# Attention output kept transposed and undivided in DRAM, divided by the output projection

## What is computed

```python
q = (x @ Wq.T + bq).reshape(b, l, h, hd).transpose(0, 2, 1, 3)      # k, v alike
scores = jnp.einsum('bhqd,bhkd->bhqk', q, k) / math.sqrt(hd)
scores = jnp.where(causal, scores, -jnp.inf)
att = jax.nn.softmax(scores, axis=-1)
out = jnp.einsum('bhqk,bhkd->bhqd', att, v)
out = out.transpose(0, 2, 1, 3).reshape(b, l, d)
return out @ Wo.T + bo                                              # x = x + this
```

## Time and profile before

| | us |
|---|---|
| median of 3 runs (1972.41 to 1987.93) | 1975.94 |
| the profiled execution's own time | 1980.81 |
| its span in the trace | 1979.0 |
| first row `mxT` written (slot 0 may start) | 169.40 |
| row `mxT` of slot 15 written | 589.19 |
| end of the last `add` of the output projection | 669.92 |
| first instruction of the MLP phase | 672.4 |

### The profile page before, as it was taken

One profiled execution on the slowest core, in us unless ns is written; L12 is line 12 of the kernel. 1 busy time (PEld: TensorE's weight loads), 2 busy tenths in 40 slices (PEclk: granted clock), 3 DMA queues, 4 the chain that ended last, 5 costly groups with the idle time before them and its releaser, 6 DMA issues.

```text
span 1979.0 us, 39339 instructions
## 1 busy us (share of the span) xinstructions
PE 1836.3 (93%) x14968; PEld 1122.2 (57%) x14968; DVE 1462.5 (74%) x2302; ACT 1031.1 (52%) x1888; POOL 760.7 (38%) x922
## 2 busy tenths in 40 slices
PE   7998888888889798999999998999999999989979
PEld 3443333333333476775775766666676766747746
DVE  6567688888873313997988988887889889969821
ACT  4234677777774123654654645636646546536411
POOL 4685656566772111223215224142151151322331
PEclk9998899999999898999999999999999999999989
DMA  7864544556434604006132331234232142071010
GB/s 237 233 198 139 153 120 126 141 140 182 142 110 118 207 1 126 12 12 188 36 125 50 81 125 41 90 81 143 68 105 73 40 133 73 12 201 33 12 40 12
DMA packets 217131, 205.68 MB, mean 104 GB/s; under 512 B 136400, under 2 KB 173264, under 8 KB 216992
## 3 DMA queue, kind: packets, MB, share of 16 engines
q1 hardware_dynamic: 210992, 187.77, 33.3%
q0 software_dynamic: 4272, 12.91, 2.0%
q10 hardware_dynamic: 1728, 3.15, 0.4%
HBM read 147.39 MB, written 33.62 MB: 91 GB/s over the span
## 4 chain that ended last, share of the span: by engine, by line
PE 51%; DVE 6%; issue 3%; POOL 3%; DMA 2%; ACT 1%; SPq 0%; DVEq 0%; ACTq 0%
PE ga L1507 12%; PE ub L1507 12%; PE acc L1517 12%; PE ga L1535 5%; PE ub L1535 5%; PE acc L1550 4%; DVE junk L1651 1%; DMA pp<-ax 1%; POOL ax L1469 1%; POOL pp L1463 1%; DVE kept L1701 1%; DVE h L1708 1%; POOL lohi L1453 1%; DMA ring<-wgu_scr 0%; DVE pat L1655 0%
## 5 line engine op out<-in xcount | busy, mean ns | idle before, releaser
L1453 POOL TENSOR_TENSOR lohi<-h,lohi 128x256 f16<-128x256 f32 x224 | 176.4, 788 | 737.8 <-ACT lohi L1598 737.6
L1587 ACT ACTIVATE kept<-ax,T 128x1376 f16<-128x1376 f32 x248 | 357.0, 1439 | 170.5 <-DVE T L1657 166.7
L1651 DVE TENSOR_SCALAR_CACHE_REDUCE junk<-ax,T 128x1376 f16<-128x1376 f32 x248 | 406.4, 1639 | 3.3
L1067 ACT ACTIVATE pr<-s 128x512 f32<-128x512 f32 (+2 forms) x640 | 320.2, 553 | 96.1 <-PE s L956 75.5
L649 DVE TENSOR_REDUCE mx<-s 128x2 f32<-128x1024 f32 (+2 forms) x300 | 319.9, 1113 | 65.3 <-PE s L628 34.7
L1507 PE MATMUL ga<-xT_f,w_gate 128*128 128x256 f16 x2688 | 332.8, 274 | 17.8 <-DVE h L1708 13.6
L1507 PE MATMUL ub<-xT_f,w_up 128*128 128x256 f16 x2688 | 332.6, 274 | 0.0
L1517 PE MATMUL acc<-w_down,lohi 128*128 128x512 f16 x1344 | 326.4, 379 | 3.9 <-POOL lohi L1453 3.9
L1507 PEld LDWEIGHTS ga<-xT_f,w_gate 128*128 128x128 f16 x2688 | 262.7, 98 | 95.0 <-DVE h L1708 21.3
L1507 PEld LDWEIGHTS ub<-xT_f,w_up 128*128 128x128 f16 x2688 | 264.3, 98 | 31.6
L1708 DVE SCALAR_TENSOR_TENSOR h<-ub,g 128x256 f32<-128x256 f32 x224 | 93.8, 419 | 155.0 <-ACT g L1593 154.0
(11 more groups left out here) (179 smaller groups left out, 2670.5 us busy)
## 6 DMA issues: line engine op xcount, KB each, us to landing
ring<-wgu_scr SPq DMA_DIRECT2D x64, 688.0 KB, 5.3
ring<-wd_scr SPq DMA_DIRECT2D x24, 768.0 KB, 6.1
wgu_scr<-tk_h POOLq DMA_DIRECT2D x32, 172.0 KB, 2.7
q_scr<-qk_h SPq DMA_DIRECT2D x16, 256.0 KB, 2.5
k_scr<-qk_h SPq DMA_DIRECT2D x16, 256.0 KB, 4.0
v_scr<-v_f SPq DMA_DIRECT2D x16, 256.0 KB, 5.1
Q<-q_scr SPq DMA_DIRECT2D x64, 64.0 KB, 2.1
K<-k_scr SPq DMA_DIRECT2D x64, 64.0 KB, 2.0
```

The costliest lines, as they stand in the source:

```text
L1067: nc.scalar.activation(pr[:, g % NPR, NP * t + p0:NP * t + p1, 0:w], scores, ACT.Exp, scale=SCALE).then_inc(e2_ok, 1)
L1453: nc.gpsimd.tensor_tensor(hT[j % 2][:, 1, :], h[j % 2][:, :], hT[j % 2][:, 0, :], ALU.subtract).then_inc(hl_ok, 1)
L1587: nc.scalar.activation(kept[0][:, :], ax[k % 2][:, 1, 0:I_TK], ACT.Sign, scale=-1.0, bias=TF[:, 1:2], accum_out=cnt[:, 1:2]).then_inc(c1_o ...
L1651: nc.vector.tensor_scalar(junk[:, :], ax[k % 2][:, 0, 0:I_TK], TF[:, 0:1], -float(KZERO), ALU.is_lt, ALU.add, accum_out=cnt[:, 0:1]).then_ ...
```

## The change

- `copy_out` no longer feeds a transpose. SP stores `oT` as it is, one DMA for each half, into `o_scr`, now (slot, 128 rows, 1024 tokens): 16 rows of undivided output and 16 of sums for each head. `output_transpose`, `divide`, `o_st` and the per-tile `rows` on PE are gone; the next half's first product waits for `copy_out` alone, and `copy_out` waits for the store of the slot before.
- For each batch and half (a quarter, q = 0 to 3) SP loads the sums of 32 heads and 512 tokens as a 128 x 128 tile (`load_sums`, four DMAs), DVE inverts it (`invert`), and SP stores the result to a new scratch `r_scr` (`store_over`, four DMAs).
- The projection goes in 8 groups of 256 tokens. `load_group` issues 16 DMAs on SP: eight load 16 partitions of output each, features on partitions, and eight load the inverses, one row broadcast to 16 partitions. DVE multiplies the two (`rows`), ACT or DVE makes the high part, DVE the low part, and PE runs the products for two tiles, now with four PSUM tiles.
- The slot's order string is another. ACT peels slot 1 off its loop and DVE slots 13 and 14, with `invert(0)` and `invert(1)` behind them.

```diff
-            def store(n):
...
+            def store(n, f):
+                sp.wait_ge(oc_ok, 2 * n + f + 1)
+                sp.dma_start(o_scr[n, :, f * BANK:(f + 1) * BANK], oT[:, f, :]).then_inc(o_out[f], 16)
...
+            def load_sums(q):
+                b, f = q // 2, q % 2
+                wait(sp, over_out[f], 16 * NSEG * b)
+                sp.wait_ge(o_out[f], 16 * GPB * (b + 1))
+                rows = o_scr[b * GPB:(b + 1) * GPB].rearrange("n (j r) t -> (n j) r t", j=QH)[:, HD, :]
+                for c in range(NSEG):
...
+                    sp.dma_start(sums[c * H:(c + 1) * H, q % 2, :], rows[:, t0:t0 + P]).then_inc(sums_in[f], 16)
+            def store_over(q):
+                b, f = q // 2, q % 2
+                sp.wait_ge(over_ok, q + 1)
+                for c in range(NSEG):
...
+                    sp.dma_start(r_scr[b, :, t0:t0 + P], sums[c * H:(c + 1) * H, q % 2, :]).then_inc(over_out[f], 16)
+            def load_group(u):
+                b, q, i = u * GW // L, u * GW // BANK, u % 2
+                wait(sp, lo_ok, u - 1)
+                sp.wait_ge(o_out[q % 2], 16 * GPB * (b + 1))
+                sp.wait_ge(over_out[q % 2], 16 * NSEG * (b + 1))
...
+                for e in range(2):
+                    for j in range(QH):
...
+                        sp.dma_start(ov[i][p, :, :], values[e, j, 0:HD, :, :]).then_inc(o_ld[i], 16)
+                        sp.dma_start(osr[i][p, :, :], over[m].unsqueeze(0).broadcast_to([HD, KB, GW])).then_inc(o_ld[i], 16)
...
             for n in range(NQ):
+                if n:
+                    store(n - 1, 1)
+                store(n, 0)
...
+                if n == NQ - 4:
+                    load_sums(0)
+                    load_sums(1)
                 if n == NQ - 2:
...
+                    store_over(0)
+                    store_over(1)
+                    load_group(0)
+                    load_group(1)
+            load_sums(2)
+            load_group(2)
+            load_group(3)
+            store_x(0)
+            store_x(1)
+            store_over(2)
+            load_group(4)
+            store_x(2)
+            store_x(3)
+            load_group(5)
+            store(NQ - 1, 1)
+            load_sums(3)
+            store_over(3)
+            for u in range(6, NGRP):
+                load_group(u)
...
             def product(t, k):
                 if k == 0:
-                    pe.wait_ge(lo_ok, t + 1)
+                    pe.wait_ge(lo_ok, t // TPG + 1)
...
-                wait(act, ot_ok, 2 * n + f - 1)
+                wait(act, o_out[f], 16 * n)
...
+            for t in range(NTILE):
+                u = t // TPG + 2
                 add(t)
+                if t == 1:
+                    invert(2)
+                if t == 5:
+                    invert(3)
+                if t % TPG and u < NGRP:
+                    rows(u)
...
-TENSOR_ORDER = "mmrmrsmrsmmssrsmrsmmsrrmsrsmmsrsmmsrsmmsrsmmsrmsmsrsmrs"
+TENSOR_ORDER = "mmrrmsmsmsmsmsmrsmmsrsmrrsmmsrsmmsrsmmsrsmmsrsmsrsmrs"
```

More of the change, by code:

```diff
@@ L719, in phase_attend @@
         XBESIDE = NDB * 3
[L720 to L721 removed]
+        pmm = [s1[i // 2][:, i % 2 * BANK:(i % 2 + 1) * BANK] for i in range(NPM)]
         va_ok = sem("va_ok")
@@ L742, in phase_attend @@
         xb_ok = sem("xb_ok")
-        tr_ok = sem("ctr_ok")
+        ov_ok = sem("cov_ok")
+        sums_in = [sem(f"sums_in{i}") for i in range(2)]
+        over_ok = sem("over_ok")
+        over_out = [sem(f"over_out{i}") for i in range(2)]
         hi_ok = [sem(f"chi_ok{i}") for i in range(2)]
@@ L773, in phase_attend @@
         order = attend_order(N1, len(pairs2), NG, end_av)
[L776 to L779, removed]
+        steps = [("product", t, k) for t in range(EARLY) for k in range(KB)]
         def last_order():
@@ L1007, in slot @@
                         products(n - 1, 1 - i, a)
-                    elif kind == "output":
-                        output_transpose(n, 0)
-                    elif kind == "output before" and not first:
-                        output_transpose(n - 1, 1)
                     elif kind == "maxima":
@@ L1079, in _ @@
             slot(0, first=True)
-            with act.Fori(1, NQ) as n:
+            slot(1)
+            with act.Fori(2, NQ) as n:
                 slot(n)
@@ L1116, in slot @@
                         sc.maxima(dve, s1, n + 1, a)
-                    elif kind == "output":
-                        divide(n, 0, h, i)
-                    elif kind == "output before" and not first:
-                        divide(n - 1, 1, h if i else h - 1, 1 - i)
                     elif kind == "maxima end":
@@ L1180, in attend_order @@
     shifted = [("shifted", v) for v in range(n2)]
-    rest = [("products before", g) for g in range(ng - TENSOR_LATE, ng)] + [("output before", 1)]
-    rest += [("products", g) for g in range(end_av[0])] + [("output", 0)]
-    rest += [("products", g) for g in range(end_av[0], ng - TENSOR_LATE)]
+    rest = [("products before", g) for g in range(ng - TENSOR_LATE, ng)]
+    rest += [("products", g) for g in range(ng - TENSOR_LATE)]
     queues = {"m": maxima, "s": shifted, "r": rest}
```

184 lines of the change are left out of this document (67 added, 117 removed).

## The result

The changed kernel took 2019.07 us (median of 4 runs, 2013.09 to 2021.59) against 1974.18 for the kernel before: ratio 1.0212, 95% interval 1.0187 to 1.0237. It is 2.1% slower. The forecast was 1983 us and its range ended at 2012.

The account below looks back on a forecast made before the run. No engine is full: PE, DVE and ACT, nearly full, hand work to each other. 1980.81 - 22.5 (slots) + 29.8 (tail) = 1988.1 us for the profiled execution, 4.9 above the median: 1983 us, range 1953 to 2012.

Parts of the forecast that it names:

- the slots: 15 slots up to the last mxT write: 1.5 us gained in each, 22.5 us in sum, bounds 12 and 45.
- the tail: From the last mxT write (called E) to the last add: 29.8 us longer, 110.5 instead of 80.7, bounds +16 and +53.
- the next slot's row is on its way as much earlier: Slot's end: with DVE earlier, the next row of maxima starts as much earlier; part of the 0.8 us gain.
- DVE sets the end of a slot: Slot's end: PE's maxima transpose waits for DVE's join and the last shifted pair queues behind it, ACT idling 0.69 us.
- the 0.8 forecast for the slot's end: Slot's end: DVE 1.4 us earlier without divisions, of which 0.8 us a slot is gained, ACT and PE then setting the pace.
- the 0.7 forecast for the first third: Slot's first third: new order saves 0.4 us of ACT's 0.62 gap, missing transposes 0.3 more; about 0.7 us a slot.
- the wait ahead of tile 0: Tail, slot 15: PE waits 13.9 us for group 0 to be loaded and split, where before it transposed at once.
- the second wait: Tail, behind tile 7: PE idle 21 us, as group 4's multiplication stands on DVE behind invert(3).
- landing of 2.1 us: Tail: a load lands 2.1 us after its issue, and the same was used for stores.
- The first (transfers): Rival, tail: narrow group loads are bound by transfer, not issue; 7 x 3.3 = 23 us more, 2006 us; chance 0.16.
- The second (clock falls): Rival, slot's first third: new string lets PE's clock fall; in the other 11 slots +44, 2027 us; chance 0.10.
- The third and fourth: Rivals: DVE alone paced the slots, 1961 or 1947 us, chance 0.15; tile 0's stall does not show, 1965 us, chance 0.07.

Follow-up runs that it names:

- e5: Changed kernel with GpSimd's weight pieces loaded half a slot later on SP, away from the write of mxT: 1998.44 us, ratio 1.0113.
- e6: Kernel before (old layout) with the weight pieces' loads likewise half a slot later: 1962.77 us, ratio 0.9929.
- e3: Changed kernel with batch 0's inverses and the loads of groups 0 and 1 one slot earlier: 2004.70 us, ratio 1.0157.
- e11: e5 with the old slot order string less its two output steps: 2002.09 us, ratio 1.0128.
- e2: Changed kernel with shifted pair 4 ahead of maxima step m6 in the order string: 2027.91 us, ratio 1.0259.
- e7: Changed kernel with the last inversion on DVE behind rows(5) instead of ahead of rows(4): 2018.12 us, ratio 1.0228.
- e8: Changed kernel with the store of slot 15's second half and the last sums' loads ahead of groups 4 and 5 on SP: 2011.35 us, ratio 1.0171.
- e9: Changed kernel with its tail rebuilt (8 loads a group, earlier inverses and groups, high parts on DVE, inversions moved), slots unchanged: 1987.57 us, ratio 1.0066.
- e12: e10 with slot 15's second store and last sums ahead of group 4, inverses' store ahead of group 5, last inversion ahead of rows(4): 1965.64 us, ratio 0.9950.
- e10: e9's rebuilt tail together with the weight pieces' loads moved as in e5, against the kernel before: 1967.26 us, ratio 0.9961.

## Why the prediction was wrong

The sum for the profiled execution was 1988.1 us; it took 2017.2. Of the 29.1 us between, 23.0 are the slots (22.5 forecast as gain, -0.5 got), 9.0 the tail (29.8 forecast, 38.8 got), -3.4 the earlier start, which is not the change's; the rest is spread thinly. Both large terms missed to the same side, and the range had been drawn as if they would not.

**The slots: the step that failed** is "the next slot's row is on its way as much earlier". The row was written earlier, but its landing did not come as much earlier: in the mean of 14 slots it landed 3.94 us behind the write of mxT, before 3.75 (in e5 and e6, with the border free, 2.72 and 2.68). Its DMA stands behind the pieces' loads, which PE's pairs release and not DVE, and in 12 of the 14 slots from the second on it came closer behind them (into slot 12, mxT is written 1.48 us after the last of these issues, before 1.73). PE waited 15.6 us for it instead of 13.1, and behind three of the longer waits the clock fell. e5 and e6 show this: with the border free the new layout gains 22.4 us and the old one 12.4, and the difference of the two layouts, hidden before, is 9.4 us over 15 slots. (These are single profiled executions; the medians of e5 and e6, less their tails of 120.8 and 77.5 us, give about 8.) So of the 22.5 us forecast, 13 were never there, and the 9.4 that were are eaten by 10.0 of collision. About 3.6 of these 10.0 are the longer waits for the row; the rest is not divided further, and the stretches at half clock lie in it.

The reading behind that step was too coarse: I took the DMA engines as 54% busy in a clean slot and costed what stands in the queue at nothing. In the four us behind mxT they were 67 to 93% busy in ten of the slots. The rows of maxima that PE waits for stood in the trace of before, 13.1 us of them, and I had looked at a slot without such a wait. The Trainium skill, "DMA: Bandwidth & Descriptors", section "Queues, rings and completion order", says that on each DMA engine descriptors are consumed in ring order, and that a completion count lands only after that engine's earlier writes. The trace agrees: 4 KB land in 1.8 us in the median with the border free, 2.8 with pieces ahead, and up to 7.0 behind 32 loads in e3, where PE waited 5.46 us.

**The size of the gain.** With the border free it is 0.6 us a slot (9.4 / 15; 0.9 in the mean of slots 3 to 15, 0.8 between the shortest slots), where I had 1.5. "DVE sets the end of a slot" was wrong as well: without the divisions but in the old order (e11) the shortest slots are some 0.1 us shorter than e6's, and DVE idles longer. So of the 0.8 forecast for the slot's end these profiles show little; the rest of the 0.8 between the shortest slots came with the new order, near the 0.7 forecast for the first third. Moving m6 ahead of pair 4 did bring a new wait on K, 1.01 us in slot 9, that I had not seen; e2 shows that the exchange back is worse. With the border free this wait stands in 14 of e5's 15 slots, 6.7 us in sum, and in one of e6's and of e11's (0.3 us); what the exchange would do there no run shows.

**The tail.** Its mechanism was right: the wait ahead of tile 0 (13.9 forecast, 15.3), half speed behind it (4 us at 0.51 of the clock, 2 us lost and not 3.6), 16 loads 0.47 apart, the second wait (21 and 23.5), DVE's passes (1.22 and 1.23), ACT's high part (1.1; DVE waited 1.19 for it). The mis-sized term is the **landing of 2.1 us**, taken from the 64 KB loads of Q and used "for stores too". It held where nothing of SP's was in flight ahead: 2.0 us for the store of slot 15's first half, 1.4 to 1.5 for the inverses of 671.93. It measured 3.8 us behind a group's last issue, 3.5 to 4.3 for the inverses of 639.43 and 5.0 for the store at 662.85. Up to these inverses SP was on time (issued by E + 55.2, forecast 55.0). What came behind them makes the 9.0 us: the landings 5, groups 4, 5 and 7, which took 8.0 to 8.7 us of SP and not 7.5, about 3, and the last two tiles, which PE began at half clock (7.04 us, the two before them 5.35), 1.8; the rest gave 1 back. ACT's high part of group 2 came 3.4 us late behind slot 15's exponentials, which I had not counted; SP's chain did not wait for it. That the second PE gap ends on DVE was right as a row and wrong as a cause: e7 removes what stands there and gains 2 us. The chain is SP's queue and its trips through DRAM, as e3, e8, e9 and e12 show by shortening it.

**The rivals.** The first (transfers) I refused for a 46% share; it was partly right. One group alone leaves the engines at 0.44 to 0.67, but a second one behind it fills them (1.13 at 123 GB/s). The Trainium skill's "SBUF — State Buffer", section "Door 1: The DMA port swizzle", which I weighed with its 104 GB/s, is nearer to this than my reading, though SP still issued groups 0 and 1 in 7.4 us each; they lay ready 10.7 and 11.2 us behind their first issues. The second (clock falls) came true in five slots. In slots 5, 7 and 14 the row was late, and in e5, with the row in time, they keep full clock. No wait length divides the slots cleanly: waits of 1.73 and 1.80 us were followed by full clock in e7. In slots 10 and 13 PE waited for no load, and such falls stay when the border is free: slots 2 and 10 of e5, 4, 7 and 11 of e10, 4 and 7 of e11 with the old string. Slot 1 falls in all of these and in e6 too, but no other of e6 does. Slot 7 of e10, 7 to 12 us behind its mxT:

```profile
338.68:343.68 5.00, 5.00 (x56) 2.01 (x60) 3.41 (x5) 2.37 (x7) 0.00 (x0) 0.67 0.97 291
```

It took 27.1 us, where the slots at full clock took 25.6 to 26.6. So in these profiles a part of the falls goes with the new layout and not with a late row. That the missing transposes leave PE too little to do there, as the rival had it, is neither shown nor ruled out; that the new string is needed for it is ruled out by e11. The cause of these falls is open. The third and fourth did not occur.

## What to carry to other kernels

A transfer that somebody waits for lands behind what is queued ahead of it, however small it is (here 4 KB: 1.7 us with the queue free, up to 4.2 behind the pieces, 7.0 behind 32 loads): read the DMA share in the few us around each hand-off, not its mean over a stage, and keep bulk loads off that place. Before an engine's time is counted as gain, follow the next hand-off to its landing; where a transfer ends the wait, as at these borders, an earlier start of the engine may bring nothing. A layout that leaves data in DRAM between stages is paid in round trips at the end, each with the queue in front of it, and an engine's largest idle stretch there may be only the shadow of that chain (23.5 us here, worth 2).

## What the hardware did that I had not expected

Two groups of loads over 16 partitions with runs of 1 KB, one behind the other, filled the DMA engines at 123 GB/s (share 1.13); loads of the same data over 128 partitions took a share of 0.61 at 213 GB/s, with a store among them. Each of the latter cost SP's queue 0.62 us, of the former 0.47. A store of 256 KB that is read back took 2.0 us to be seen with nothing of SP's ahead of it, 3.7 in e12, and with a group's 1 MB ahead 5.0 in the changed kernel and 7.4 in e10. PE's clock fell to half in slots in which PE had not waited for the row (0.66 in slot 10 of the changed kernel and of e5, 0.67 in slot 7 of e10). The reciprocal of 128x128 took 0.95 us.
